# Masking the inner attention scores on VectorE instead of TensorE, in a banded attention with a product-key feed-forward

## The chip, the cores and the metric

The kernel runs on one core of a Trainium2 chip. The metric is the device time of one execution in microseconds (us): before the change, the median of three runs is 1780.42 us (1779.67 to 1784.23).

## What is computed

The reference normalizes x (16 sequences of 512 rows, 128 wide), runs attention with 16 heads of width 8 in which a query sees only keys at most 128 rows away, adds the residual, and runs a second layer (batch norm, product keys, the top 8 of 64 candidates, expert rows weighted by a softmax). Only the attention bears on the change:

```python
x = L0_attn_x
x = x + _L0_attn_ref(_layernorm(x, axis=-1), w_qkv, w_proj)
x = x + _L0_ffn_ref(_layernorm(x, axis=-1), ...)
# in _L0_attn_ref:
attn = jnp.einsum('bhqd,bhkd->bhqk', q, k) / math.sqrt(DK)
mask = jnp.abs(idx[None, :] - idx[:, None]) > WINDOW      # WINDOW = 128
attn = jnp.where(mask[None, None], -1000000000.0, attn)
p = jax.nn.softmax(attn, axis=-1)
out = jnp.einsum('bhqk,bhkd->bhqd', p, v)
```

## The kernel before

The program has two stages, one behind the other: `attention`, and then `ffn`, which the change leaves alone.

A sequence has four tiles of 128 queries. With a band of 128, the first and the last query tile see two tiles of keys each (the outer scores, PSUM tile SX, 2 x 256 columns), and the two inner ones see three tiles each (the inner scores, PSUM tile SY, 2 x 384 columns). Each of SX and SY has one buffer.

The attention is a pipeline over sequences. In the step of sequence c, a loop over the 16 heads does, for each head, on each engine in a fixed order written by hand:

- TensorE: `scores` of sequence c (SX, then SY), some of the single products and transposes that the list SHARED gives to heads (they share the one bank MB), for four of the 16 heads (2, 6, 10, 14 by VSLOT) the product with the values, `values` (16 pairs of matmuls, PV), and then `scoresT` of sequence c-1, the transposed scores less their row's maximum (TX, TY).
- VectorE: the maximum of each row of SX (L409) and of SY (L411), and between them the small work that belongs to that head: statistics and normalization (L378 to L388), the splitting of q and k into three bf16 parts (L435, L440), the division by the sums (L447, L449), the residual (L457), and the batch-norm statistics (L468).
- ScalarE: the exponentials of TX and TY (L354, L356) and copies out of MB.
- GpSimd: zeroes the entries outside the band after the exponential (L264) and computes two small powers (L272, L286).
- SP: the DMAs; q and k go through DRAM and come back, spread over partitions.

Masking of the scores that the maxima are taken of is done on TensorE. After the product of a tile, a further matmul adds a triangle of -1e30 (`bandb`, bf16) through the identity `idb`. SX needs one such matmul of 256 columns, SY four of 128 columns (two for each query tile, L492):

```python
for n, i in enumerate((1, 2)):
    tile(SY[:, n, 0:3 * P], i, i - 1, i + 2)
    outside(SY[:, n, 0:P], LO)
    o = outside(SY[:, n, 2 * P:3 * P], HI)
o.then_inc(S["inner_scores"], 1)
```

`scores` of a head waits for `outer_maxima` of the head before (SX free), and then, before SY, for `inner_maxima` of the head before (SY free). VectorE waits for `outer_scores` ahead of L409 and for `inner_scores` ahead of L411. TensorE's two transposes of the maxima (L559, L563) wait for `inner_maxima`, and the bank MB passes from one user to the next by `bank_free`.

Steps -1, 0 and 1 and steps 14 to 17 are written out; steps 2 to 13 are the body of a hardware loop of six turns, two steps in each:

```python
for t in (-1, 0, 1):
    do(t, t)
with eng.Fori(0, 6) as i:
    do(i * 2 + 2, 2)
    do(i * 2 + 3, 3)
```

Of the kernel before, what the change touches and what calls it, by code (L numbers as in the profile page):

```python
# [33 lines left out]
P = 128  # L34
# [15 lines left out]
VSUB = TILES * H // 2 * SLOT_V  # L50


def attention(nc, ctx, x, w_qkvT, w_projT, identb, band, w_q, keysT, idf, bnst, KM, extra, x1_out, x2T_out, first):
    def sb(name, shape, dt=F32):
        return ctx.enter_context(nc.sbuf_tensor(name, shape, dt))

# [17 lines left out]
    KT = sb("KT", [P, 2 * FH * NK])  # L74
    idb = sb("idb", [P, P], BF16)
    bandb = sb("bandb", [P, 2 * P], BF16)
    xin = [sb(f"xin{b}", [P, TILES, P]) for b in range(2)]
    xres = sb("xres", [P, TILES, P])
    st6 = sb("st6", [P, TILES, 6])
# [46 lines left out]


    def steps(eng, do):
        for t in (-1, 0, 1):
            do(t, t)  # L130
        with eng.Fori(0, 6) as i:
            do(i * 2 + 2, 2)
            do(i * 2 + 3, 3)
        for t in (14, 15, 16, 17):
            do(t, t)


# [31 lines left out]
    def _(sp):  # L169

        sp.dma_start(xin[0][:, :, :], xs[0]).then_inc(S["x_loaded"], 16)
        for dst, src in ((wq[:, :], w_qkvT), (wp[:, :], w_projT), (idb[:, :], identb), (bandb[:, :], band)):
            sp.dma_start(dst, src).then_inc(S["consts_loaded"], 16)
        for dst, src in extra[:1]:
            sp.dma_start(dst, src).then_inc(S["consts_loaded"], 16)
# [196 lines left out]
    def _(dve):  # L372
# [18 lines left out]
        def shift(s, nth):  # L391
# [4 lines left out]
            dve.wait_ge(S["max_part2"], s * 2 + nth)  # L396
            nc.vector.tensor_tensor(mp[:, 2, :], rm[:, :], mp[:, 1, :], ALU.subtract).then_inc(S["max_part3"], 1)

        def step(t, c):
            b = c % 2  # L400
            for h in range(H):
                if 0 <= c < SEQS:
                    n = t * H + h + 1
                    dve.wait_ge(S["outer_scores"], n)
                    if h == 0 and c >= 1:
                        dve.wait_ge(S["maxima_turned"], t * 2 - 1)
                    if h == 8 and c >= 1:
                        dve.wait_ge(S["maxima_turned"], t * 2)
                    nc.vector.tensor_reduce(mx[:, h, 0:4:3], SX[:, :, :], AX.X, ALU.max).then_inc(S["outer_maxima"], 1)  # L409
                    dve.wait_ge(S["inner_scores"], n)  # L410
                    nc.vector.tensor_reduce(mx[:, h, 1:3], SY[:, :, 0:384], AX.X, ALU.max).then_inc(S["inner_maxima"], 1)  # L411

                if h == 1 and 0 <= c - 1 < SEQS:
                    shift(t - 1, 2)
                if h == 9 and 0 <= c < SEQS:
                    shift(t, 1)

                if h == 0 and 0 <= c + 1 < SEQS:
                    dve.wait_ge(S["x_loaded"], 16 * (t + 2))
                    stats(0, t + 1, xin[1 - b], st6, mv, ve, S["x_stats"], S["x_means"], S["x_variance"])  # L420
                if h == 1 and 0 <= c + 1 < SEQS:
                    stats(1, t + 1, xin[1 - b], st6, mv, ve, S["x_stats"], S["x_means"], S["x_variance"])
                if h == 3 and 0 <= c + 1 < SEQS:
                    dve.wait_ge(S["x_rstd"], t + 2)
                    if c >= 0:
                        dve.wait_ge(S["xn_turned"], t + 1)
                    norm(xin[1 - b], mv, rs, xn, S["xn_ready"])
                if c == -1 and h in (4, 7):

                    both = K[0 if h == 4 else 1][64:P, :, :].rearrange("p h n -> p (h n)").bitcast(F32)  # L430
                    nc.vector.memset(both, TWO_ONES).then_inc(S["k_ones_set"], 1)
                for hh, nm, dst, r, sc in ((5, "q", qp, rq, DK ** -0.5), (7, "k", kp, rk, 1.0)):
                    if h == hh and 0 <= c + 1 < SEQS:
                        dve.wait_ge(S[nm + "_part1"], t + 2)
                        nc.vector.scalar_tensor_tensor(out=r[:, :].rearrange("p (i n) -> p i n", n=P), in0=MB[:, :, :], scalar=sc,  # L435
                                                       in1=dst[:, 0, :].rearrange("p (i n) -> p i n", n=P),
                                                       op0=ALU.mult, op1=ALU.subtract).then_inc(S[nm + "_rest"], 1)
                    if h == hh + 1 and 0 <= c + 1 < SEQS:
                        dve.wait_ge(S[nm + "_part2"], t + 2)
                        nc.vector.tensor_tensor(dst[:, 2, :], r[:, :], dst[:, 1, :], ALU.subtract).then_inc(S[nm + "_part3"], 1)  # L440

                for i, sl in enumerate(ASLOT):
                    if h == sl and 0 <= c - 2 < SEQS:
                        n = (t - 2) * 2 + i + 1
                        dve.wait_ge(S["att_turned"], n)
                        hv = MB[:, :, :].rearrange("p g (h e) -> p (g h) e", e=SLOT_V // 2)
                        nc.vector.reciprocal(rec[:, i, :], hv[:, :, DK]).then_inc(S["sums_inverted"], 1)  # L447
                        dve.wait_ge(S["sums_inverted"], n)
                        nc.vector.tensor_tensor(A[:, 2 * i:2 * i + 2, :].rearrange("p i (h d) -> p (i h) d", d=DK), hv[:, :, 0:DK],  # L449
                                                rec[:, i, :].unsqueeze(2).broadcast_to([P, 2 * H, DK]), ALU.mult).then_inc(S["att_normed"], 1)  # L450

                if h == 12 and 0 <= c - 2 < SEQS:
                    dve.wait_ge(S["projected"], t - 1)
                    dve.wait_ge(S["residual_loaded"], 16 * (t - 1))
                    if c - 2 >= 1:
                        dve.wait_ge(S["x1_stored"], 16 * (t - 2))
                    nc.vector.tensor_tensor(X1[:, :, :], MB[:, :, :], xres[:, :, :], ALU.add).then_inc(S["x1_ready"], 1)  # L457
                if h == 13 and 0 <= c - 2 < SEQS:
                    dve.wait_ge(S["x1_ready"], t - 1)
                    stats(0, t - 2, X1, t6, tv, te, S["x1_stats"], S["x1_means"], S["x1_variance"])  # L460
                    stats(1, t - 2, X1, t6, tv, te, S["x1_stats"], S["x1_means"], S["x1_variance"])
                if h == 14 and 0 <= c - 2 < SEQS:
                    dve.wait_ge(S["x1_rstd"], t - 1)
                    norm(X1, tv, trs, X2, S["x2_ready"])
# [6 lines left out]

    @block.tensor
    def _(pe):
        pe.wait_ge(S["consts_loaded"], 80)
        pe.wait_ge(S["v_pads_set"], 5)

        HI, LO = bandb[:, 0:P], bandb[:, P:2 * P]

        def scores(t, c, h):

# [3 lines left out]
            if h == 8:  # L484
                pe.wait_ge(S["heads_8_15_loaded"], 192 * (t + 1))

            def tile(out, i, k0, k1, clear=True):
                pe.matmul(out, Q[b][0:KQ, h, i * P:(i + 1) * P], K[b][0:KQ, h, k0 * P:k1 * P],  # L488
                          start=clear, stop=False, skip_group_check=True)

            def outside(out, band_):
                return pe.matmul(out, idb[:, :], band_, start=False, stop=True, skip_group_check=True)  # L492

            if c > 0 or h > 0:
                pe.wait_ge(S["outer_maxima"], n - 1)
            tile(SX[:, 0, :], 0, 0, 2)
            tile(SX[:, 1, :], 3, 2, 4, False)

            outside(SX[:, :, :].rearrange("p j n -> p (j n)")[:, P:3 * P], bandb[:, :]).then_inc(S["outer_scores"], 1)
            if c > 0 or h > 0:  # L500
                pe.wait_ge(S["inner_maxima"], n - 1)
            for n, i in enumerate((1, 2)):
                tile(SY[:, n, 0:3 * P], i, i - 1, i + 2)
                outside(SY[:, n, 0:P], LO)
                o = outside(SY[:, n, 2 * P:3 * P], HI)
            o.then_inc(S["inner_scores"], 1)

        def scoresT(t, c, h):

# [40 lines left out]
        def step(t, c):  # L550
            b = c % 2
            for h in range(H):
# [2 lines left out]

                if h == 1 and 0 <= c - 1 < SEQS:
                    bank_free(pe, "mt1", t, c)
                    pe.wait_ge(S["inner_maxima"], t * H)
                    pe.transpose(MB[0:HT, 0, :], mx[:, 8:16, :].rearrange("p h i -> p (h i)"), idf[:, :]).then_inc(S["maxima_turned"], 1)  # L559
                if h == 9 and 0 <= c < SEQS:  # L560
                    bank_free(pe, "mt0", t, c)
                    pe.wait_ge(S["inner_maxima"], t * H + 8)
                    pe.transpose(MB[0:HT, 0, :], mx[:, 0:8, :].rearrange("p h i -> p (h i)"), idf[:, :]).then_inc(S["maxima_turned"], 1)  # L563

                if h == 4 and 0 <= c + 1 < SEQS:
# [447 lines left out]
        outputs(GROUPS * GT - 1, GROUPS - 1, 1, GT - 1)  # L1013


def program(nc, x, w_qkvT, w_projT, ident, identb, band, w_q, keysT, key_inT, key_out, gb, out):
    x1 = nc.dram_tensor("x1", (SEQS * T, P), F32, kind="Internal").ap()
    x2T = nc.dram_tensor("x2T", (P, SEQS * T), F32, kind="Internal").ap()
    with ExitStack() as both:
# [9 lines left out]
        first = [sb("X1_first", [P, TILES, P]), sb("X2T_first", [P, T])]  # L1029
        extra = [(idf[:, :], ident), (KI[:, :], key_inT), (KO[:, :, :], key_out), (GB[:, :], gb)]  # L1030
        with ExitStack() as ctx:
            attention(nc, ctx, x, w_qkvT, w_projT, identb, band, w_q, keysT, idf, bnst, KM, extra, x1, x2T, first)
        with ExitStack() as ctx:
            ffn(nc, ctx, x1, x2T, KM, KI, KO, GB, idf, bnst, first, out)

# [35 lines left out]
```

## Time and profile before

| what | value |
|---|---|
| median of three runs | 1780.42 us |
| the profiled execution | 1781.27 us, its span 1779.6 us |
| TensorE busy | 1539.2 us (86%), 11712 matmuls |
| VectorE busy | 1477.4 us (83%) |
| ScalarE busy | 1266.0 us (71%) |
| GpSimd busy | 1328.7 us (75%) |
| mean granted TensorE clock | 0.953 of full speed |

PE is TensorE's matmuls, PEld its weight loads, DVE VectorE, ACT ScalarE, POOL GpSimd, SPq the queue that issues the DMAs. A row `[x <-E T Lnnn]` says that the engine stood idle for x us before the instruction, until line nnn of engine E, which writes T, had ended. The busy time of a matmul runs from its start to a modelled end, so that matmuls in a row overlap; what one takes from its successor is seen from start to start. VectorE's instructions also overlap by a little. The attention fills the first 780 us of the span, the feed-forward the rest.

### The profile page before, as it was taken

What the parts mean: (1) busy time and instruction counts of PE and PEld (TensorE: products, weight loads), DVE (VectorE), ACT (ScalarE), POOL (GpSimd) and SP (SyncE); (2) the same over time, 40 slices, a digit from 0 to 9 for tenths busy, and PEclk for the clock granted to TensorE, in tenths of its full rate; (3) what the DMA queues carried; (4) which work ended last, traced back from release to release, by engine and by line L of the source; (5) the groups of instructions that cost most, each with busy time, mean ns of one, the idle gap of its engine ahead of it and who ended that gap; (6) DMA issues with size and microseconds to landing.
All of it is one profiled execution on the core that took longest, in us unless ns stands there. A gap on an engine that the chain in (4) does not pass through costs nothing.

```text
span 1779.6 us, 35628 instructions
## 1 busy us (share of the span) xinstructions
PE 1539.2 (86%) x11712; PEld 1100.6 (62%) x11712; DVE 1477.4 (83%) x3720; ACT 1266.0 (71%) x1741; POOL 1328.7 (75%) x1579
## 2 busy tenths in 40 slices
PE   3899999999999999868888888888888888888887
PEld 2455655656555665426666676766666676766666
DVE  3767888888878887339999999999999999999998
ACT  1156666666666666638888888888888888888885
POOL 1045555555555555639999999999999999999993
PEclk9789999999999999969999999999999999999999
DMA  5334444444444443010000000000000000000000
GB/s 143 78 82 93 101 101 99 100 97 97 97 97 105 97 97 84 27 54 1 19 18 2 19 19 1 19 19 19 1 19 19 9 10 19 19 1 19 13 7 7
DMA packets 73436, 85.62 MB, mean 48 GB/s; under 512 B 9856, under 2 KB 63616, under 8 KB 68608
## 3 DMA queue, kind: packets, MB, share of 16 engines
q1 hardware_dynamic: 73312, 84.08, 20.1%
q8 instruction: 64, 1.05, 0.3%
q14 instruction: 60, 0.49, 0.1%
HBM read 58.10 MB, written 25.95 MB: 47 GB/s over the span
## 4 chain that ended last, share of the span: by engine, by line
POOL 31%; issue 7%; DVE 7%; ACT 6%; PE 5%; DVEq 0%; ACTq 0%; SPq 0%
POOL SUM L746 31%; DVE W L939 5%; PE WT L1007 3%; ACT E L847 3%; ACT L781 1%; PE MB L949 1%; ACT GE L780 1%; DVE M8Y L883 0%; PE MB L952 0%; DVE SMALL L900 0%; ACT SIM L774 0%; PE MB L974 0%; DVE CT L922 0%; PE E L962 0%; ACT OUT L794 0%
## 5 line engine op out<-in xcount | busy, mean ns | idle before, releaser
L746 POOL TENSOR_TENSOR SUM<-SIM 128x1024 f32<-128x1024 f32 x512 | 958.0, 1913 | 9.5 <-DVE W L939 5.5
L939 DVE SCALAR_TENSOR_TENSOR W<-SUM,SMALL,E 128x1024 f32<-128x1024 f32 x512 | 641.6, 1279 | 45.8 <-ACT E L847 43.8
L847 ACT ACTIVATE E<-SUM,NB 128x1024 f32<-128x1024 f32 x512 | 566.8, 1118 | 100.1 <-DVE W L939 89.8
L1007 PEld LDWEIGHTS WT<-idf,W 128*128 128x128 f32 x4096 | 488.7, 149 | 237.9 <-DVE W L939 124.3
L1007 PE MATMUL WT<-idf,W 128*128 128x128 f32 x4096 | 559.9, 288 | 70.8 <-DVE CT L922 38.0
L264 POOL TENSOR_SCALAR_AFFINE_SELECT PT<-PT 128x128 f32<-128x128 f32 (+1 forms) x1024 | 334.6, 351 | 319.4 <-ACT PT L354 283.0
L409 DVE TENSOR_REDUCE mx<-SX 128x2 f32<-128x512 f32 x256 | 175.3, 685 | 105.1 <-PE SX L492 104.3
L411 DVE TENSOR_REDUCE mx<-SY 128x2 f32<-128x768 f32 x256 | 242.4, 947 | 7.3 <-PE SY L492 6.9
L354 ACT ACTIVATE PT<-TX 128x512 f32<-128x512 f32 x256 | 152.9, 597 | 98.5 <-PE TX L519 97.1
L356 ACT ACTIVATE PT<-TY 128x768 f32<-128x768 f32 x256 | 207.2, 809 | 1.5
L488 PE MATMUL SY<-K,Q 72*128 72x384 bf16 x512 | 164.0, 343 | 16.4 <-DVE mx L411 15.7
L545 PE MATMUL PV<-PT,V 128*32 128x384 f32 (+1 forms) x2048 | 154.7, 444 | 2.3 <-POOL PT L264 2.3
L492 PE MATMUL SY<-bandb,idb 128*128 128x128 bf16 x1024 | 146.7, 225 | 0.0
L949 PE MATMUL MB<-KM,BNT 128*128 128x512 f32 x128 | 79.5, 706 | 70.9 <-ACT OUT L794 69.1
L519 PE MATMUL TY<-Q,K 75*128 75x384 bf16 x512 | 127.2, 330 | 6.2 <-ACT PT L356 6.2
L492 PEld LDWEIGHTS SY<-bandb,idb 128*128 128x128 bf16 x1024 | 104.1, 102 | 40.5 <-issue 6.4
L974 PE MATMUL MB<-KO,CT 128*128 128x128 f32 x1024 | 124.9, 275 | 1.1 <-DVE CT L922 1.1
L974 PEld LDWEIGHTS MB<-KO,CT 128*128 128x128 f32 x1024 | 119.5, 192 | 1.3 <-DVE CT L922 1.3
L488 PE MATMUL SX<-K,Q 72*128 72x256 bf16 x512 | 103.1, 284 | 14.2 <-DMA Q<-q_parts 12.4
L545 PEld LDWEIGHTS PV<-PT,V 128*32 128x32 f32 x2048 | 60.8, 111 | 72.8 <-issue 53.5
L519 PE MATMUL TX<-Q,K 75*128 75x256 bf16 x512 | 100.3, 277 | 5.1 <-DMA Q<-m_parts 3.5
L922 DVE TENSOR_TENSOR CT<-WT,GE 128x1024 f32<-128x1024 f32 x64 | 78.3, 1224 | 17.6 <-PE WT L1007 17.6
(111 smaller groups left out, 1663.3 us busy)
## 6 DMA issues: line engine op xcount, KB each, us to landing
K<-k_parts SPq DMA_DIRECT2D x96, 192.0 KB
Q<-q_parts SPq DMA_DIRECT2D x288, 64.0 KB
q_parts<-qp SPq DMA_DIRECT2D x16, 384.0 KB, 2.4
k_parts<-kp SPq DMA_DIRECT2D x16, 384.0 KB, 2.4
xin<-in_x SPq DMA_DIRECT2D x16, 256.0 KB, 3.1
xres<-in_x SPq DMA_DIRECT2D x16, 256.0 KB, 9.4
x<-X SPq DMA_DIRECT2D x16, 256.0 KB, 2.2
x2T<-X2T SPq DMA_DIRECT2D x16, 256.0 KB, 2.1
```

Source lines behind the costliest of these rows:

```text
L264: return nc.gpsimd.affine_select(out=out, in_=out, compare_op=ALU.is_ge, fill=0.0, base=0, pattern=([[0, 2]] if pairs else []) + [[s, P]], ...
L356: nc.scalar.activation(pt[:, 512:1280].rearrange("p (j n) -> p j n", j=2), TY[:, :, 0:384], ACT.Exp).then_inc(S["inner_exp"], 1)
L411: nc.vector.tensor_reduce(mx[:, h, 1:3], SY[:, :, 0:384], AX.X, ALU.max).then_inc(S["inner_maxima"], 1)
L488: pe.matmul(out, Q[b][0:KQ, h, i * P:(i + 1) * P], K[b][0:KQ, h, k0 * P:k1 * P], start=clear, stop=False, skip_group_check=True)
L492: return pe.matmul(out, idb[:, :], band_, start=False, stop=True, skip_group_check=True)
L519: return pe.matmul(out[:, 0:(q1 - q0) * P], K[b][0:R, h, j * P:(j + 1) * P], Q[b][0:R, h, q0 * P:q1 * P], start=True, stop=True, skip_grou ...
L545: o = pe.matmul(PV[32 * e:32 * e + 32, q0 * P:q1 * P], V[b][:, slot:slot + SLOT_V], PT[:, h % 8, at:at + (q1 - q0) * P], start=(j == 0 and ...
L746: return eng.tensor_tensor(SUM[(q * FH + h) % RING][:, :].rearrange("p (i j) -> p i j", i=NK), sx, sy, ALU.add)
L847: nc.scalar.activation(E[h % 2][:, :], SUM[(k * FH + h) % RING][:, :], ACT.Exp, bias=NB[q][:, h:h + 1]).then_inc(S["exp_ready"], 1)
L939: nc.vector.scalar_tensor_tensor(out=W[h % WRING][:, :], in0=SUM[(k * FH + h) % RING][:, :], scalar=TOP[q][:, h, TOPK - 1:TOPK], in1=E[h % ...
L974: o = pe.matmul(po, CT[k % 2][:, e, :], key_out[:, e, :], start=False, stop=(e == BLK - 1))
L1007: o = pe.matmul(WT[:, e, :], W[h % WRING][:, e * P:(e + 1) * P], ident[:, :], is_transpose=True, start=(h == 0 and e % 4 == 0), stop=(h == ...
```

## The change

- The four matmuls that add the triangles to SY are gone. The product of each of the two inner query tiles now ends its own group and raises `inner_scores` by itself, so that this semaphore goes up twice for a head.
- VectorE's L411, one maximum over both inner tiles, becomes two `tensor_tensor_reduce`, one for each tile: the instruction adds a mask `bandf` (fp32, SBUF, 384 columns: triangle, zeros, triangle) to the scores, writes the sum back to SY, and leaves the row's maximum in `mx`. Each waits for its own tile and raises `inner_maxima`, which now also goes up twice; `scores` waits for each half of SY by itself.
- `bandf` is a new constant of 128 x 384 fp32, loaded with the other constants; TensorE and VectorE wait for all six of them (96) where TensorE waited for five (80).
- All steps of the attention are written out; the hardware loop is gone.

SX keeps its mask matmul and its L409.

```diff
+    bandf = sb("bandf", [P, 3 * P])
...
     def steps(eng, do):
-        for t in (-1, 0, 1):
-            do(t, t)
-        with eng.Fori(0, 6) as i:
-            do(i * 2 + 2, 2)
-            do(i * 2 + 3, 3)
-        for t in (14, 15, 16, 17):
+        for t in range(-1, SEQS + 2):
             do(t, t)
...
-        for dst, src in ((wq[:, :], w_qkvT), (wp[:, :], w_projT), (idb[:, :], identb), (bandb[:, :], band)):
+        for dst, src in ((wq[:, :], w_qkvT), (wp[:, :], w_projT), (idb[:, :], identb), (bandb[:, :], band), (bandf[:, :], bands)):
             sp.dma_start(dst, src).then_inc(S["consts_loaded"], 16)
...
+        def masked_max(scores, k0, k1, out):
+
+            return nc.vector.tensor_tensor_reduce(out=scores, in0=scores, in1=bandf[:, k0 * P:k1 * P], scale=1.0,
+                                                  scalar=-3e38, op0=ALU.add, op1=ALU.max, accum_out=out)
+
+        dve.wait_ge(S["consts_loaded"], 96)
...
-                    dve.wait_ge(S["inner_scores"], n)
-                    nc.vector.tensor_reduce(mx[:, h, 1:3], SY[:, :, 0:384], AX.X, ALU.max).then_inc(S["inner_maxima"], 1)
+                    dve.wait_ge(S["inner_scores"], 2 * n - 1)
+                    masked_max(SY[:, 0, 0:3 * P], 0, 3, mx[:, h, 1:2]).then_inc(S["inner_maxima"], 1)
+                    dve.wait_ge(S["inner_scores"], 2 * n)
+                    masked_max(SY[:, 1, 0:3 * P], 0, 3, mx[:, h, 2:3]).then_inc(S["inner_maxima"], 1)
...
-        pe.wait_ge(S["consts_loaded"], 80)
+        pe.wait_ge(S["consts_loaded"], 96)
...
-            if c > 0 or h > 0:
-                pe.wait_ge(S["inner_maxima"], n - 1)
-            for n, i in enumerate((1, 2)):
-                tile(SY[:, n, 0:3 * P], i, i - 1, i + 2)
-                outside(SY[:, n, 0:P], LO)
-                o = outside(SY[:, n, 2 * P:3 * P], HI)
-            o.then_inc(S["inner_scores"], 1)
...
+            for e, i in enumerate((1, 2)):
+                if c > 0 or h > 0:
+                    pe.wait_ge(S["inner_maxima"], 2 * n - 3 + e)
+                tile(SY[:, e, 0:3 * P], i, i - 1, i + 2).then_inc(S["inner_scores"], 1)
...
-                    pe.wait_ge(S["inner_maxima"], t * H)
+                    pe.wait_ge(S["inner_maxima"], t * H * 2)
...
-                    pe.wait_ge(S["inner_maxima"], t * H + 8)
+                    pe.wait_ge(S["inner_maxima"], t * H * 2 + 16)
```

## Rows read from the trace of the kernel before

**Rows 1.** The page: busy time of each engine, and the granted clock in 40 slices

```profile
PE 1539.2 (86%) x11712; PEld 1100.6 (62%) x11712; DVE 1477.4 (83%) x3720; ACT 1266.0 (71%) x1741; POOL 1328.7 (75%) x1579
...
PEclk9789999999999999969999999999999999999999
```

**Rows 2.** Busy time by stretch: window, length, busy us (instructions), clock, DMA share, GB/s

```profile
80.00:124.00 44.00, 42.24 (x324) 25.61 (x322) 30.57 (x54) 25.27 (x43) 20.67 (x63) 0.82 0.37 81
...
218.84:261.90 43.06, 40.25 (x382) 25.71 (x378) 35.05 (x73) 26.65 (x47) 22.88 (x67) 1.00 0.45 99
```

**Rows 3.** Timeline of GpSimd, one fixed instruction of three successive steps: start, us, instruction

```profile
596.83 1.01 POOL L286 TENSOR_TENSOR trs<-te,half 128x4 f32<-128x4 f32 x1
...
639.88 1.01 POOL L286 TENSOR_TENSOR trs<-te,half 128x4 f32<-128x4 f32 x1
...
682.92 1.01 POOL L286 TENSOR_TENSOR trs<-te,half 128x4 f32<-128x4 f32 x1
```

**Rows 4.** Timeline of VectorE in one looped step

```profile
433.48 0.38 DVE L382 BATCH_NORM_AGGREGATE mv<-st 128x2 f32<-128x6 f32 x4
...
436.81 0.69 DVE L409 TENSOR_REDUCE mx<-SX 128x2 f32<-128x512 f32 x1 [1.25 <-PE SX L492]
...
439.72 0.42 DVE L449 TENSOR_TENSOR A<-MB,rec 128x256 f32<-128x256 f32 x1
...
448.05 0.69 DVE L409 TENSOR_REDUCE mx<-SX 128x2 f32<-128x512 f32 x1 [1.25 <-PE SX L492]
...
450.15 0.69 DVE L435 SCALAR_TENSOR_TENSOR rk<-MB,kp 128x512 f32<-128x512 f32 x1 [0.55 <-ACT kp L313]
450.75 0.68 DVE L409 TENSOR_REDUCE mx<-SX 128x2 f32<-128x512 f32 x1
451.35 0.95 DVE L411 TENSOR_REDUCE mx<-SY 128x2 f32<-128x768 f32 x1
452.22 0.68 DVE L440 TENSOR_TENSOR kp<-rk,kp 128x512 bf16<-128x512 f32 x1
...
453.54 0.68 DVE L409 TENSOR_REDUCE mx<-SX 128x2 f32<-128x512 f32 x1
...
459.18 0.69 DVE L409 TENSOR_REDUCE mx<-SX 128x2 f32<-128x512 f32 x1 [1.80 <-PE SX L492]
...
462.56 0.69 DVE L457 TENSOR_TENSOR X<-MB,xres 128x512 f32<-128x512 f32 x1
463.44 0.69 DVE L409 TENSOR_REDUCE mx<-SX 128x2 f32<-128x512 f32 x1 [0.18 <-PE SX L492]
...
468.67 1.12 DVE L388 TENSOR_SCALAR X<-X,tv,trs 128x128 f32<-128x128 f32 x4 [0.58 <-POOL trs L286]
...
474.25 0.67 DVE L409 TENSOR_REDUCE mx<-SX 128x2 f32<-128x512 f32 x1
474.84 0.95 DVE L411 TENSOR_REDUCE mx<-SY 128x2 f32<-128x768 f32 x1
```

**Rows 5.** Timeline of TensorE in the same step

```profile
440.27 0.65 PE L569 MATMUL MB<-idf,xn 128*128 128x128 f32 x4 [1.07 <-DVE A L449]
...
453.68 0.28 PE L563 MATMUL MB<-idf,mx 128*32 128x128 f32 x1 [0.59 <-DVE A L449]
...
455.14 0.34 PE L488 MATMUL SY<-K,Q 72*128 72x384 bf16 x1 [0.30 <-DVE mx L411]
455.31 0.28 PE L492 MATMUL SY<-bandb,idb 128*128 128x128 bf16 x2
455.43 0.33 PE L488 MATMUL SY<-K,Q 72*128 72x384 bf16 x1
...
475.85 0.34 PE L488 MATMUL SY<-K,Q 72*128 72x384 bf16 x1 [0.36 <-DVE mx L411]
```

**Rows 6.** Timeline of the start: a constant's DMA issue, and TensorE's first work

```profile
2.79 0.43 SPq L173 DMA_DIRECT2D bandb<-in_band  x1
...
7.71 1.09 PE L569 MATMUL MB<-idf,xn 128*128 128x128 f32 x4 [7.71 <-DVE xn L388]
```

More of the change, by code:

```diff
@@ L50, with attention @@
 VSUB = TILES * H // 2 * SLOT_V
-def attention(nc, ctx, x, w_qkvT, w_projT, identb, band, w_q, keysT, idf, bnst, KM, extra, x1_out, x2T_out, first):
+def attention(nc, ctx, x, w_qkvT, w_projT, identb, band, bands, w_q, keysT, idf, bnst, KM, extra, x1_out, x2T_out, first):
     def sb(name, shape, dt=F32):
@@ L473, in _ @@
     def _(pe):
-        pe.wait_ge(S["consts_loaded"], 80)
+        pe.wait_ge(S["consts_loaded"], 96)
         pe.wait_ge(S["v_pads_set"], 5)
-        HI, LO = bandb[:, 0:P], bandb[:, P:2 * P]
         def scores(t, c, h):
@@ L485, in scores, with tile @@
                 pe.wait_ge(S["heads_8_15_loaded"], 192 * (t + 1))
[L487 to L492, printed above, removed]
+            def tile(out, i, k0, k1, clear=True, done=True):
+                return pe.matmul(out, Q[b][0:KQ, h, i * P:(i + 1) * P], K[b][0:KQ, h, k0 * P:k1 * P],
+                                 start=clear, stop=done, skip_group_check=True)
             if c > 0 or h > 0:
                 pe.wait_ge(S["outer_maxima"], n - 1)
-            tile(SX[:, 0, :], 0, 0, 2)
-            tile(SX[:, 1, :], 3, 2, 4, False)
-            outside(SX[:, :, :].rearrange("p j n -> p (j n)")[:, P:3 * P], bandb[:, :]).then_inc(S["outer_scores"], 1)
-            if c > 0 or h > 0:
-                pe.wait_ge(S["inner_maxima"], n - 1)
-            for n, i in enumerate((1, 2)):
-                tile(SY[:, n, 0:3 * P], i, i - 1, i + 2)
-                outside(SY[:, n, 0:P], LO)
-                o = outside(SY[:, n, 2 * P:3 * P], HI)
-            o.then_inc(S["inner_scores"], 1)
+            tile(SX[:, 0, :], 0, 0, 2, done=False)
+            tile(SX[:, 1, :], 3, 2, 4, clear=False, done=False)
+            pe.matmul(SX[:, :, :].rearrange("p j n -> p (j n)")[:, P:3 * P], idb[:, :], bandb[:, :],
+                      start=False, stop=True, skip_group_check=True).then_inc(S["outer_scores"], 1)
+            for e, i in enumerate((1, 2)):
+                if c > 0 or h > 0:
+                    pe.wait_ge(S["inner_maxima"], 2 * n - 3 + e)
+                tile(SY[:, e, 0:3 * P], i, i - 1, i + 2).then_inc(S["inner_scores"], 1)
         def scoresT(t, c, h):
@@ L1013, in _, with program @@
         outputs(GROUPS * GT - 1, GROUPS - 1, 1, GT - 1)
-def program(nc, x, w_qkvT, w_projT, ident, identb, band, w_q, keysT, key_inT, key_out, gb, out):
+def program(nc, x, w_qkvT, w_projT, ident, identb, band, bands, w_q, keysT, key_inT, key_out, gb, out):
     x1 = nc.dram_tensor("x1", (SEQS * T, P), F32, kind="Internal").ap()
@@ L1031, in program @@
         with ExitStack() as ctx:
-            attention(nc, ctx, x, w_qkvT, w_projT, identb, band, w_q, keysT, idf, bnst, KM, extra, x1, x2T, first)
+            attention(nc, ctx, x, w_qkvT, w_projT, identb, band, bands, w_q, keysT, idf, bnst, KM, extra, x1, x2T, first)
         with ExitStack() as ctx:
@@ L1056 @@
         "band": np.concatenate([np.where(keep.T, 0, -1e30), np.where(keep, 0, -1e30)], axis=1).astype(ml_dtypes.bfloat16),
+        "bands": np.concatenate([np.where(keep, 0, -1e30), np.zeros((P, P)), np.where(keep.T, 0, -1e30)], axis=1).astype(np.float32),
         "w_q": np.asarray(L0_ffn_w_q),
```

## The prediction

> **What bounds the kernel now.** I read the page first: TensorE is busy for 86% of the span, VectorE for 83%, and no engine stands out [rows 1]. The change touches only the attention, so I cut that stage into windows. A steady step of it takes 43.06 us, of which TensorE is busy for 40.25 and VectorE for 35.05, at full clock [rows 2]. Neither fills the step, so the next views are the timelines of both engines in one step, to see who waits for whom. They take turns. Ahead of L409 of heads 3, 7 and 11 (at 436.81, 448.05 and 459.18) VectorE stands idle for 1.25, 1.25 and 1.80 us until TensorE has the outer scores [rows 4]; these are the heads behind the long product with the values. In other places TensorE stands idle until VectorE is done: 1.07 us at L569, 0.59 at L563, 0.30 and 0.36 at the first tile of SY [rows 5]. The step is thus a chain that changes engines: pieces that go by VectorE's work and pieces that go by TensorE's.
>
> **The price of each part.**
>
> TensorE loses four matmuls for each head. Two of them stand between 455.31 and 455.43, 0.12 us from start to start, with rounding 0.115 [rows 5]. That is 0.23 us a head, 3.7 us in a step of 16 heads, where TensorE's is the piece that counts. Its busy time of 0.28 for the pair is not the price.
>
> VectorE trades one maximum over 768 columns for two masked ones over 384. L409 with 512 columns takes 0.60 us from its start to the next start (450.75 to 451.35), L411 with 768 takes 0.87 (451.35 to 452.22) [rows 4]. The slope is 0.27 us for 256 columns, so 384 columns take 0.60 - 0.135 = 0.465. Two make 0.93, which is x = 0.06, say 0.07 us a head more than L411. The second source, in SBUF, costs nothing by L457, which reads PSUM and SBUF and lasts 0.69 for 512 columns, as L409 does [rows 4]. No row shows an operation that writes a tensor and a maximum besides, so that I bound it. Below: nothing, x = 0.07. A likely value: one more small instruction for each. Four of L382 last 0.38 us in all, a single one some 0.16, so that they start (0.38 - 0.16) / 3 = 0.075 apart [rows 4]; x = 0.07 + 0.15 = 0.22. Above: the small instruction starts only when the masked one has quite ended (0.08 later, since L409 lasts 0.68 and its successor starts after 0.60), and runs its 0.16 out: x = 2 x (0.465 + 0.08 + 0.16) - 0.87 = 0.54. I take 0.22, because VectorE's instructions without a wait between them overlap throughout rows 4. The Trainium skill speaks against the change here: "VectorE: DVE Perf Modes", section "Two Vector instructions with no wait between them", treats an op that also writes out its accumulator as two instructions. No run here shows it yet; by that rule x = 0.22 or more, without it 0.07 and some 20 us less in all.
>
> Nor does a row show VectorE reading and writing one PSUM bank in the same instruction. If a column then took two cycles, x would be 0.22 + 2 x 384 x 1.05 ns = 1.03. The outputs of L409, L411 and L457 go to SBUF. This end is kept as a rival.
>
> Now along the chain of one step, with x for each head on a VectorE piece and -0.23 on a TensorE piece [rows 4, 5]:
>
> - 436.81 to 440.27, head 3: VectorE's L409, L411, norms, L449, and then TensorE's L569: +x = +0.22.
> - 440.27 to 448.05: TensorE's; the masks of heads 5 and 6 fall out: -0.46.
> - 448.05 to 453.54: at head 7, L435 waits 0.55 us for a product that stands behind head 7's masks: -0.23; head 8 is VectorE's: +x. Together -0.01.
> - 453.54 to 459.18: the first tile of SY waits for L411 (455.14), and behind it stand both tiles and four masks. Now the first tile is filled while VectorE reads the second half, and only one tile (0.17) is left behind the second. That saves 0.23 for the masks and 0.17 or 0.18 for the tile: x - 0.41 = -0.19.
> - 459.18 to 463.44, heads 11 and 12: TensorE's, -0.46; but VectorE's own work there is 4.26 less the waits ahead of the two L409, 0.4 and 0.25, so that with 2x it takes 4.05. It becomes the bound: -0.20.
> - 463.44 to 475.85, heads 13 to 1: VectorE's. Head 14 hides its x under the 0.58 us for which L388 waits for GpSimd; heads 13, 15, 0 and 1 pay: +4x; some 0.2 of a wait for a copy at head 15 goes, as TensorE is earlier; at 475.85 the tiles of SY gain 0.41 as above: 4x - 0.61 = +0.27.
>
> The sum is -0.37 us a step, with x = 0.22. For the 14 steps of sequences 2 to 15 that makes -5.2 us. In general the pieces add up to 9x - 2.35, which is zero at x = 0.26: the change stands close to where it turns. With x = 0.07 heads 11 and 12 stay TensorE's, and the sum is -1.68 a step, -23.5 us; with 0.54 L435 of head 7 is no longer earlier either, and it is +2.7, +38 us.
>
> Sequences 0 and 1 run in part at a lower clock: the stretch from 80 to 124 had 0.82 of full speed [rows 2], which is full speed for some of it and half for the rest. There a mask costs twice as much, 0.46 us a head, and TensorE is busy 42.24 of 44.00. For some ten heads at half clock, 4.6 us, and x against it in about seven others, 1.5, I put -3 us.
>
> The new constant is 192 KB, one more DMA issue, 0.48 us behind the others on SP's queue, and TensorE waits for it. Its first work was at 7.71, released by VectorE's norms, while the issue of `bandb` was done at 3.22 [rows 6]; two more issues and the landing come close to that. I put +0.5, between 0 and 1.5. The loads of xin and of the feed-forward's tables are one issue later too; their first use comes later, so nothing.
>
> Writing out the steps costs or gives nothing. The instruction L286 of successive steps stands at 596.83, 639.88 and 682.92: the last looped step took 43.05, the first written-out one 43.04 [rows 3]. The second stage is the same. The Trainium skill, "Runtime: NRT & Kernel Launch", section "Instruction fetch mechanics", says that a taken branch can force a fetch and that kernels prefer full unrolling; the trace shows no such gain here, 0.01 us a step, 0.1 us in all.
>
> The sum: -5.2 - 3 + 0.5 = -7.7 against the profiled 1781.27 us, whose span was 1779.6. The median of the runs is 0.85 lower: 1780.42 - 7.7 = 1772.7, say 1773 us.
>
> **The rivals.**
>
> The second output is dear. VectorE would have x from 0.3 to 0.54, if the write of the maximum doesn't overlap with its neighbours. For it: three ALU steps and two outputs in one instruction, an operation no row shows. Against it: everything small on VectorE overlaps. It decides from x = 0.26 upward; at 0.4 the sum is +1.3 us a step, 1780.4 + 18 - 2.5 = 1796; at 0.54, 1816. Chance 0.20. This is the one that ends on the other side.
>
> The bank's two accesses halve the rate. VectorE's 35 us of a step would become 35 + 16.5 = 51.5, the bound of every head, 52 with waits: +9 for 16 steps, 1925 us. Chance 0.05.
>
> The clock falls. TensorE has 3.7 us less to do in a step and stands idle more often. Now it holds full speed in each steady step [rows 2], but the page's slices at the start, in which it works less, show 7 and 8 [rows 1]. If some 3 us of each step ran at half speed on a TensorE piece, that would be +1.5 a step, +21: 1794 us. Chance 0.10.
>
> The second output is free, x = 0.07: 1780.4 - 23.5 - 3 + 0.5 = 1754 us. Chance 0.12.
>
> The change does nothing: what VectorE takes and TensorE gives cancel, since a wait gone on one engine comes back at the next (the waits for ScalarE and GpSimd stay). 1778 us. Chance 0.08.
>
> **How the numbers follow.** My forecast, x from 0.15 to 0.28, has 0.45, and the time 1773. Its own range is 1764 to 1779. The measurement tells changes from about 0.3%, 5.3 us, so the forecast is faster below 1775.1: 0.35 of its 0.45, and 0.10 within. With the free output that makes 0.47 faster; within 0.3% come 0.10, 0.08 for nothing, and 0.03 from the edge of the rivals: 0.21; slower is the rest, 0.32. The range of 1757 to 1803 leaves out the half rate, the upper part of the dear output and some of the free one, 2 in 10 in all.
>
> **What would show it.** In the trace after: 1024 matmuls less in all; the pair of masked maxima taking 1.09 us from the start of the first to the start of what follows (0.87 now; 0.94 if the second output is free, over 1.2 if it is dear, 1.9 at half rate); L409's waits at heads 3, 7 and 11 still there; L569's wait longer (1.07 + 0.45), because VectorE is now later and TensorE earlier; a steady step of 42.7 us; clock 1.00 in it; the written-out steps alike. I am wrong if the pair's price is outside 0.93 to 1.15, if a steady step shows a lower clock, or if heads 4, 11 and 12 turn into VectorE's and the small TensorE savings vanish.

## The result, and the profile after

The changed kernel takes 1801.12 us (median of 15 runs, 1782.63 to 1805.96) against 1780.01 us (15 runs); the ratio is 1.0097, with a 95% interval of 1.0075 to 1.0118. It is slower, by 1%. I had forecast 1773 us, and faster. The measured time lies within the stated range, but the change moved the time the other way. Ratios here compare runs in the usual state alone; one of the ten runs of half_masks took 2418 us at a granted clock of 0.56 and is left out of its ratio.

The profiled execution took 1802.2 us, its span 1800.5, which is 20.9 us more than before. The page, as in [rows 1]:

```profile
PE 1540.5 (86%) x10688; PEld 1049.4 (58%) x10688; DVE 1509.5 (84%) x4488; ACT 1264.7 (70%) x1741; POOL 1334.4 (74%) x1579
...
PEclk9679999899989999878999999999999999999999
```

TensorE has 1024 matmuls less and is busy for as long as before. That is the sign to stop at. In the row of the clock the attention's slices, all 9 before once the start was over, now show 8 here and there: TensorE was granted full speed for a part of the time only.

What VectorE's new instructions take, from its timeline at head 8 of a step (start, us, instruction), beside L409, L411 and L440 of [rows 4], which are L412, L397 and L445 now:

```profile
280.95 0.68 DVE L412 TENSOR_REDUCE mx<-SX 128x2 f32<-128x512 f32 x1
281.55 0.56 DVE L397 CUSTOM_DVE_ANT_0 SY<-SY,bandf 128x384 f32<-128x384 f32 x1
282.02 0.14 DVE L397 DVE_READ_ACCUMULATOR2_ANT mx<- 128x1 f32 x1
282.02 0.60 DVE L397 CUSTOM_DVE_ANT_0 SY<-SY,bandf 128x384 f32<-128x384 f32 x1
282.54 0.14 DVE L397 DVE_READ_ACCUMULATOR2_ANT mx<- 128x1 f32 x1
282.54 0.69 DVE L445 TENSOR_TENSOR kp<-rk,kp 128x512 bf16<-128x512 f32 x1
```

The pair takes 282.54 - 281.55 = 0.99 us from start to start; L411 took 0.87. So x is 0.12 us a head. The maximum is written out by an instruction of its own (0.14 us). That is as the Trainium skill has it ("VectorE: DVE Perf Modes", section "Two Vector instructions with no wait between them"): an op with an accumulator output is two instructions. But it runs beside the next one: each of them starts when its successor starts. The first masked maximum takes 0.47 us to the next start, the second 0.52, so that the cost beyond the rate of a plain maximum is some 0.05 us.

How long the steps are, by GpSimd's L282 (L286 of [rows 3]) in two parts of the stage:

```profile
389.07 1.01 POOL L282 TENSOR_TENSOR trs<-te,half 128x4 f32<-128x4 f32 x1
430.72 1.01 POOL L282 TENSOR_TENSOR trs<-te,half 128x4 f32<-128x4 f32 x1
474.04 1.01 POOL L282 TENSOR_TENSOR trs<-te,half 128x4 f32<-128x4 f32 x1
518.40 1.01 POOL L282 TENSOR_TENSOR trs<-te,half 128x4 f32<-128x4 f32 x1
...
607.71 1.01 POOL L282 TENSOR_TENSOR trs<-te,half 128x4 f32<-128x4 f32 x1
652.10 1.01 POOL L282 TENSOR_TENSOR trs<-te,half 128x4 f32<-128x4 f32 x1
697.05 1.01 POOL L282 TENSOR_TENSOR trs<-te,half 128x4 f32<-128x4 f32 x1
```

Steps of 41.65, 43.32, 44.36, 44.39 and 44.95 us: one kernel, written-out steps with the same instructions, 3.3 us apart. Before, they were 43.05 and 43.04 [rows 3]. The windows of the first and of the third of these steps say what differs (columns as in [rows 2]; the clock stands behind the last count):

```profile
389.07:430.72 41.65, 37.80 (x322) 21.59 (x314) 37.06 (x121) 26.52 (x46) 23.32 (x68) 1.00 0.46 104
474.04:518.40 44.36, 40.69 (x321) 22.47 (x314) 36.67 (x120) 26.55 (x46) 23.32 (x67) 0.92 0.43 99
```

At full speed a step takes 41.65 us, 1.4 less than before. With a mean clock of 0.92, which is some 7 of the 44.36 us at half speed (1.2 GHz instead of 2.4), it takes 2.7 us more than that. Of the twelve steps between the first and the last row of this kind (167.91 and 697.05), the one at 389.07 alone had the clock at 1.00; two had 0.96 and nine 0.92.

The last three rows of GpSimd stand 10.9, 12.2 and 14.1 us behind those of before [rows 3]. The 20.9 us of the span are thus 1.7 up to the first of these rows, 12.4 in the twelve steps, 4.3 in the last steps of the attention and 2.5 in the feed-forward. Of the last two little is the change's: in the last steps both_masks and before_flat (below), at the time of the kernel before, are 3.3 and 1.9 us longer too, and before_flat is 2.4 longer in the feed-forward.

Where the half speed bites is seen on both engines' timelines around head 10 of a slow step (from 255.63 to 300.04). TensorE:

```profile
284.00 0.28 PE L561 MATMUL MB<-idf,mx 128*32 128x128 f32 x1 [0.93 <-DVE A L454]
284.12 0.57 PE L517 MATMUL TX<-Q,K 75*128 75x256 bf16 x2
284.50 0.84 PE L517 MATMUL TY<-Q,K 75*128 75x384 bf16 x2
...
286.55 4.50 PE L543 MATMUL PV<-PT,V 128*32 128x256 f32 x32
290.98 0.39 PE L517 MATMUL TX<-Q,K 75*128 75x256 bf16 x2
```

and VectorE:

```profile
286.30 0.67 DVE L412 TENSOR_REDUCE mx<-SX 128x2 f32<-128x512 f32 x1
...
292.07 0.69 DVE L412 TENSOR_REDUCE mx<-SX 128x2 f32<-128x512 f32 x1 [4.05 <-PE SX L499]
```

Behind its wait of 0.93 us TensorE goes on at half speed (the pair of TX lasts 0.57 where it lasts 0.39 at 290.98), and the product with the values, the longest piece that is TensorE's alone, takes 4.50 us. VectorE, which waited 1.80 us at this place before [rows 4], waits 4.05. The same instructions in the step at full speed, with a values product of head 6 in front:

```profile
408.59 2.36 PE L543 MATMUL PV<-PT,V 128*32 128x256 f32 x32
...
417.45 0.28 PE L561 MATMUL MB<-idf,mx 128*32 128x128 f32 x1 [0.93 <-DVE A L454]
417.57 0.38 PE L517 MATMUL TX<-Q,K 75*128 75x256 bf16 x2
```

The product takes 2.36 us there. The wait of 0.93 us is the same to the hundredth, and this time the speed stays, so that no single wait decides.

### The profile page after: what moved, and what is told of

The parts are those of the page before. It is cut to its first block, busy times and chain, and to the rows that moved or that the text cites. A ratio compares the mean times of both kernels' runs of the same rounds, so it can differ in the third digit from the quotient of the medians.

```text
span 1800.5 us, 33004 instructions
## 1 busy us (share of the span) xinstructions
PE 1540.5 (86%) x10688; PEld 1049.4 (58%) x10688; DVE 1509.5 (84%) x4488; ACT 1264.7 (70%) x1741; POOL 1334.4 (74%) x1579
## 4 chain that ended last, share of the span: by engine, by line
POOL 41%; issue 5%; ACT 4%; DVE 3%; PE 2%; DVEq 0%; ACTq 0%; SPq 0%
POOL SUM L744 41%; DVE W L937 2%; ACT E L845 2%; ACT L779 1%; PE WT L1005 1%; ACT GE L778 1%; PE MB L947 0%; PE MB L972 0%; PE E L960 0%; DVE M8Y L881 0%; DVE SMALL L898 0%; ACT L778 0%; DVE CT L920 0%; ACT SIM L772 0%; PE MB L950 0%
## 5 line engine op out<-in xcount | busy, mean ns | idle before, releaser
L1005 PEld LDWEIGHTS WT<-idf,W 128*128 128x128 f32 x4096 | 494.3, 151 | 234.2 <-DVE W L937 120.7
L1005 PE MATMUL WT<-idf,W 128*128 128x128 f32 x4096 | 566.3, 291 | 69.4 <-DVE CT L920 38.0
L260 POOL TENSOR_SCALAR_AFFINE_SELECT PT<-PT 128x128 f32<-128x128 f32 (+1 forms) x1024 | 340.2, 357 | 328.9 <-ACT PT L350 293.1
L397 DVE CUSTOM_DVE_ANT_0 SY<-SY,bandf 128x384 f32<-128x384 f32 x512 | 273.9, 576 | 0.0
L412 DVE TENSOR_REDUCE mx<-SX 128x2 f32<-128x512 f32 x256 | 175.1, 684 | 106.2 <-PE SX L499 105.7
L543 PE MATMUL PV<-PT,V 128*32 128x384 f32 (+1 forms) x2048 | 177.7, 495 | 2.3 <-POOL PT L260 2.3
L491 PE MATMUL SY<-K,Q 72*128 72x384 bf16 x512 | 152.2, 356 | 6.9 <-DVE mx L397 6.1
L517 PE MATMUL TY<-Q,K 75*128 75x384 bf16 x512 | 132.6, 342 | 6.9 <-ACT PT L352 6.7
L543 PEld LDWEIGHTS PV<-PT,V 128*32 128x32 f32 x2048 | 66.0, 122 | 100.2 <-issue 86.5
L491 PEld LDWEIGHTS SX<-K,Q 72*128 72x128 bf16 x512 | 49.9, 102 | 69.9 <-DVE mx L412 21.3
L491 PEld LDWEIGHTS SY<-K,Q 72*128 72x128 bf16 x512 | 52.2, 102 | 55.6 <-DVE mx L397 48.4
```

The lines of the kernel that those rows point to most:

```text
L260: return nc.gpsimd.affine_select(out=out, in_=out, compare_op=ALU.is_ge, fill=0.0, base=0, pattern=([[0, 2]] if pairs else []) + [[s, P]], ...
L397: return nc.vector.tensor_tensor_reduce(out=scores, in0=scores, in1=bandf[:, k0 * P:k1 * P], scale=1.0, scalar=-3e38, op0=ALU.add, op1=ALU ...
L491: return pe.matmul(out, Q[b][0:KQ, h, i * P:(i + 1) * P], K[b][0:KQ, h, k0 * P:k1 * P], start=clear, stop=done, skip_group_check=True)
L517: return pe.matmul(out[:, 0:(q1 - q0) * P], K[b][0:R, h, j * P:(j + 1) * P], Q[b][0:R, h, q0 * P:q1 * P], start=True, stop=True, skip_grou ...
L543: o = pe.matmul(PV[32 * e:32 * e + 32, q0 * P:q1 * P], V[b][:, slot:slot + SLOT_V], PT[:, h % 8, at:at + (q1 - q0) * P], start=(j == 0 and ...
L1005: o = pe.matmul(WT[:, e, :], W[h % WRING][:, e * P:(e + 1) * P], ident[:, :], is_transpose=True, start=(h == 0 and e % 4 == 0), stop=(h == ...
```

## The experiments

Theory 1, formed on this profile: the change does what it should in the chain, but it takes so much work from TensorE that it is granted half speed in most steps, and that costs more than the chain gains. Theory 2: the masked maxima are what costs, VectorE sets the steps. All runs are timed against the kernel before on the same chip.

**The masks put back, beside the masked maxima (both_masks).**

```diff
-                tile(SY[:, e, 0:3 * P], i, i - 1, i + 2).then_inc(S["inner_scores"], 1)
+                tile(SY[:, e, 0:3 * P], i, i - 1, i + 2, done=False)
+                pe.matmul(SY[:, e, 0:P], idb[:, :], bandb[:, P:2 * P], start=False, stop=True, skip_group_check=True)
+                pe.matmul(SY[:, e, 2 * P:3 * P], idb[:, :], bandb[:, 0:P], start=False, stop=True,
+                          skip_group_check=True).then_inc(S["inner_scores"], 1)
```

> The changed kernel, with the four mask matmuls of each head put back ahead of the masked maxima (the mask is then added twice, with the same maxima). TensorE has the work of before, VectorE that of the changed kernel. Theory 1, the clock: the changed kernel is slow because TensorE, with less work, is granted half speed for 6.8 us in most steps. With the masks back the clock stays at 1.00 in the steady steps, and the kernel gets faster though it does more: steady step 43.5 us, time 1785 to 1790. Theory 2, VectorE: the masked maxima cost 0.24 us a head more, and that sets the step. Then more work can't help: steady step 44.4 or more, time 1801 or above.

1781.67 us, ratio 1.0007 (0.9993 to 1.0022). A step in the windows:

```profile
292.17:335.21 43.04, 40.55 (x382) 25.98 (x378) 37.27 (x121) 26.60 (x46) 23.30 (x68) 1.00 0.47 102
```

A kernel that does strictly more than the changed one is 1% faster, with the clock at 1.00 in all twelve steps. Theory 2 is out. And beside TensorE's old work the masked maxima cost hardly anything: 43.04 us a step, where before_flat, the next run, has 42.94.

**Written-out steps alone (before_flat).** The edit is the change's second hunk, on the kernel before.

> The kernel before with all steps written out and nothing else. As predicted, no effect: steady step 43.05 us at clock 1.00, ratio 1.000 within 0.003. If writing out were what changed the granted clock, half-speed stretches would show in the steady steps here too, and the time would be near 1800.

1781.0 us, ratio 0.9999 (0.9986 to 1.0012).

```profile
336.57:379.51 42.94, 40.31 (x382) 25.70 (x378) 34.95 (x73) 26.58 (x46) 22.92 (x67) 1.00 0.45 102
```

No effect on the time, none on the clock. The step is 0.1 us shorter than the looped one, some 1.4 us in twelve steps, which the total doesn't show.

**TensorE's relief alone (no_inner_mask).** On the written-out kernel before:

```diff
             for n, i in enumerate((1, 2)):
-                tile(SY[:, n, 0:3 * P], i, i - 1, i + 2)
-                outside(SY[:, n, 0:P], LO)
-                o = outside(SY[:, n, 2 * P:3 * P], HI)
+                o = pe.matmul(SY[:, n, 0:3 * P], Q[b][0:KQ, h, i * P:(i + 1) * P], K[b][0:KQ, h, (i - 1) * P:(i + 2) * P],
+                              start=True, stop=True, skip_group_check=True)
             o.then_inc(S["inner_scores"], 1)
```

> The kernel before, written out, with the four mask matmuls of each head left out and the maximum taken by the one reduction of before: the maximum runs over all three key tiles, inside the band or not (softmax allows any shift). VectorE's price is thus nothing, TensorE's relief is that of the changed kernel. Theory 1: TensorE is idle more often than before, half-speed stretches appear in steady steps here as well; at full clock a step would be 40.5 to 41, with the stretches 42.5 to 43.5, time 1765 to 1785. Theory 2: no clock effect, the whole relief is seen: step 41 us at most in every step, time 1750 or below.

1775.01 us (1766.74 to 1791.78), ratio 0.9967 (0.9934 to 1.0000). Five of the twelve steps had the full clock, the others took 42.7 to 45.9 us. One of each:

```profile
338.26:379.31 41.05, 37.13 (x321) 21.12 (x314) 34.83 (x73) 26.46 (x46) 23.11 (x67) 1.00 0.45 106
251.33:297.21 45.88, 42.06 (x322) 22.90 (x314) 34.98 (x73) 26.71 (x46) 23.06 (x68) 0.89 0.44 96
```

The half speed comes without any masked maximum, once TensorE has less to do. But this kernel is no slower than the one before: in its profiled execution five steps kept the full clock, against one in the changed kernel, and why the masked maxima make that worse is not shown. With before_flat and both_masks this takes the full-clock step apart: relief alone 42.94 to 41.05, -1.89 us; the masked maxima alone +0.10; both 41.65, so that beside the relief the maxima, with the waits that come in two halves, cost 0.60.

**Half of the masks (half_masks).** The changed kernel, with the two mask matmuls put back for the first inner tile only (`e == 0`).

> The changed kernel with the two mask matmuls of the first inner tile put back, those of the second left out: TensorE's work stands half-way between the changed kernel and the run with all four back. At full clock a step should take 42.3 us (between 41.65 and 43.03). Theory 1: half-speed stretches are rarer than in the changed kernel but not gone, time 1780 to 1795. Theory 2, without a clock effect: half-way between 1801 and 1781, 1791, with clock 1.00.

1776.3 us, ratio 0.9977 (0.9961 to 0.9993).

```profile
335.92:377.84 41.92, 38.56 (x354) 24.07 (x350) 37.11 (x121) 26.58 (x46) 23.13 (x67) 1.00 0.47 102
250.39:294.00 43.61, 40.49 (x354) 24.36 (x350) 37.10 (x121) 26.58 (x46) 23.09 (x68) 0.96 0.44 101
```

The half speed is rarer and shorter (0.96 for 0.92 in an affected step, and nine of the twelve steps have none). The total is lower than I expected of theory 1, and lower than that of either neighbour: less work than before, and little of the clock lost.

**Matmuls of zeros where TensorE waits (fill_idle, fill_more).** A matmul of zeros into PV, without a start flag, adds nothing:

```diff
+        def fill(n):
+            for _ in range(n):
+                pe.matmul(PV[:, :], ZB[:, 0:P], ZB[:, :], start=False, stop=True, skip_group_check=True)
...
                 if h == 9 and 0 <= c < SEQS:
+                    if c >= 2:
+                        fill(4)
                     bank_free(pe, "mt0", t, c)
...
                 if h == 4 and 0 <= c + 1 < SEQS:
+                    if c >= 2:
+                        fill(6)
                     bank_free(pe, "xnT", t, c)
```

> The changed kernel, with matmuls of zeros into PV (512 columns each, they add nothing) where TensorE waits for VectorE anyway: six at head 4 (it waits 1.5 us there) and four at head 9 (1.1 us). Theory 1: the half-speed stretch at head 10 goes or gets rarer, steady step 41.7 us where the clock is 1.00; if it goes in all steps, 14 steps x 2.8 us less, time about 1765. Theory 2: no gain, 1801, as these matmuls shorten nothing.

1779.84 us (1771.93 to 1787.24), ratio 0.9988 (0.9969 to 1.0008). Two of its steps:

```profile
434.38:476.02 41.64, 39.68 (x330) 22.42 (x324) 37.04 (x121) 26.41 (x46) 23.46 (x67) 1.00 0.46 106
256.24:303.13 46.89, 43.56 (x331) 23.89 (x324) 37.25 (x121) 26.64 (x46) 23.47 (x67) 0.89 0.46 96
```

Better than the changed kernel by 1%, but not what I expected if theory 1 held in all steps: five of the twelve steps had the full clock. Half speed was gone from head 10 and came up in heads 0 to 2. In the slow step above it set in behind two waits for DMAs that bring back parts of Q from DRAM, 0.78 us and then 1.80, both at head 0, and took in the values product of head 2:

```profile
263.14 0.61 PE L523 MATMUL TX<-Q,K 75*128 75x256 bf16 x2 [1.80 <-DMA Q<-m_parts]
...
268.16 4.36 PE L549 MATMUL PV<-PT,V 128*32 128x256 f32 x32
```

That step is 5.2 us longer than the other, but the two waits are in it besides the clock. The second run spreads the zeros:

```diff
+FILL = {15: 2, 0: 2, 1: 2, 4: 6, 8: 2, 9: 4}
...
                 if 0 <= c < SEQS:
                     scores(t, c, h)
+                    if c >= 1:
+                        fill(FILL.get(h, 0))
```

> The changed kernel with matmuls of zeros into PV (512 columns each, they add nothing) from sequence 1 on, at each head at which TensorE was seen to wait for VectorE: two each at heads 15, 0, 1 and 8, six at head 4, four at head 9, behind the scores; 18 in a step, about 3.8 us of TensorE. With ten at heads 4 and 9 alone the half-speed stretches became rarer and moved to heads 15 to 1. Theory 1, the clock: they go from the steady steps, the step is 41.6 to 42.2 us, clock 1.00, time 1760 to 1768. Theory 2, TensorE's added work eats what the clock gives: step 43, time 1780.

1762.97 us (four runs), ratio 0.9898 (0.9874 to 0.9921), and the steps are those of the chain:

```profile
414.66:456.29 41.63, 40.76 (x337) 23.08 (x332) 37.04 (x121) 26.52 (x46) 23.43 (x67) 1.00 0.48 103
```

18 matmuls added to each step, 38 us of the median gone. One steady step of the profiled execution still had a half-speed stretch (45.9 us); it too has two waits for these DMAs ahead of it, of 0.66 and 1.13 us. The other eleven took 41.6 to 41.8.

**The control: the same zeros where the clock is full anyway (before_fill).** The written-out kernel before with the 18 matmuls.

> A control: the kernel before, written out, with its masks and with the same 18 matmuls of zeros in a step. Its steady steps had full speed already. If the zeros help only through the clock, they can give nothing here, and the step grows by what of them isn't hidden: 43.0 to 44.0, time 1780 to 1795. If they helped in another way (order, waits), this kernel would get faster too, by some 1%.

1786.15 us, ratio 1.0018 (1.0002 to 1.0034):

```profile
380.23:423.60 43.37, 42.93 (x397) 27.76 (x396) 34.90 (x73) 26.59 (x46) 22.81 (x67) 1.00 0.45 100
```

The step is 0.43 us longer than without them. Where the clock is full anyway the zeros give nothing. In fill_more they left the full-clock step as it was (41.63 for 41.65) and raised the share of such steps from one to eleven in twelve, so that their gain there is the clock's.

**Faster than both kernels (nomask_fill, nomask_fill_early, nomask_all_fill).** The maximum in a softmax may be any number near the largest score, so that the mask isn't needed for it as long as no score outside the band is so far above those inside that every exponential of the row becomes zero; inputs of that kind were not run. The kernel without inner masks got the 18 matmuls:

> The kernel before, written out, without the four mask matmuls (the maximum over all three key tiles by one reduction), with the same 18 matmuls of zeros. Without them a step took 41.05 us at full clock and 44.3 to 45.9 with a half-speed stretch. Theory 1: clock 1.00 in the steady steps, step 41.1 to 41.8, time 1752 to 1762. Theory 2: 1775 to 1780.

1753.11 us (four runs, 1751.15 to 1760.60), ratio 0.986 (0.9828 to 0.9892), with all twelve steps at clock 1.00.

```profile
405.92:446.99 41.07, 40.13 (x336) 22.95 (x332) 34.86 (x73) 26.52 (x46) 23.09 (x68) 1.00 0.46 108
```

Then zeros at the start too, `elif c == 0 and h >= 8: fill(4)`:

> As the one before, and in the step of sequence 0 four more matmuls of zeros behind the scores of heads 8 to 15, where TensorE ran at half speed and waited for VectorE and for the loads of q and k. Theory 1: the clock is at full speed earlier in the step of sequence 1, 2 to 5 us less than the run without them. Theory 2: they only lengthen head by head at half speed (0.43 us each), 5 us more.

1758.69 us (four runs, 1753.60 to 1764.36), ratio 0.9882 (0.9847 to 0.9916): no gain, and the intervals overlap. The first of GpSimd's rows, L285 here, stood at 163.1 us, 4 us later than without them. But it was not the added matmuls that took these 4 us, as theory 2 had it. Of the values products behind them, first in nomask_fill, then in nomask_fill_early:

```profile
116.91 2.36 PE L548 MATMUL PV<-PT,V 128*32 128x256 f32 x32
126.38 2.36 PE L548 MATMUL PV<-PT,V 128*32 128x256 f32 x32
...
116.58 2.36 PE L548 MATMUL PV<-PT,V 128*32 128x256 f32 x32
129.38 3.33 PE L548 MATMUL PV<-PT,V 128*32 128x256 f32 x32
```

At 117 us the kernel with the zeros was 0.3 us ahead; then a half-speed stretch came, which the other execution had not (clock 0.73 and 1.00 from 120 to 130 us). The start differs by 2 or 3 us between executions of the same instructions, half speed included (next section), so that this pair doesn't tell what the zeros at the start are worth. And without the mask of the outer scores (its matmul of 256 columns left out, `outer_scores` raised by the second tile):

> The fastest so far (no mask matmuls on the inner scores, one plain maximum, 18 matmuls of zeros), and in addition the mask matmul of the outer scores left out: its maximum too runs over keys outside the band. TensorE is relieved by another 0.11 us a head. If the clock holds, the step is 40.5 to 40.9 us (41.07 with that mask), time 1743 to 1750; if the lower load brings the half-speed stretches back, 1755 to 1765.

1750.51 us (four runs, 1749.38 to 1751.34), ratio 0.9816 (0.9788 to 0.9844), the fastest. The interval touches that of nomask_fill, so the order of these two isn't settled. Two of its steps:

```profile
442.93:484.24 41.31, 38.98 (x317) 21.56 (x316) 35.03 (x73) 26.55 (x46) 23.00 (x67) 1.00 0.48 105
524.94:565.64 40.70, 38.96 (x317) 21.56 (x316) 34.94 (x73) 26.54 (x46) 23.04 (x67) 1.00 0.49 107
```

The clock was full in all twelve. Nine took 40.7 us; in the three of 41.3 to 42.5 TensorE waits 1.3 to 1.4 us for the DMA that fills Q from `m_parts` (0.9 at most in the others), so that at this speed the reload begins to show.

## Why the prediction was wrong

**The step that failed** is the sentence on the clock. I counted every steady step at full speed, as before, and gave the falling clock a chance of 0.10. It was the case that came: eleven of the twelve steady steps ran in part at half speed. My price for it was right in kind and low: 3 us of each step at half speed, +1.5, 1794 us; the trace shows about 7 us in an affected step, +2.7, and 1801 us. I had the sign of it in hand: the start, in which TensorE gets fewer matmuls done (324 in 44.00 us, where a steady step has 382), ran in part at half speed [rows 1, 2], and the change takes 3.7 us of work, by my price, from the 40.25 of a step and makes TensorE wait longer for VectorE. What I took as evidence against, full speed in every steady step, only said that the old load was enough. That 1801 us lies within my range of 1757 to 1803 is no merit of the forecast: the upper part of it stood for a dear second output, which didn't come.

**VectorE's price.** x = 0.22 was forecast, with 0.07 and 0.54 as the ends; it is 0.12. The rate of the plain maximum held (0.47 us from start to start for 384 columns, as worked out from L409 and L411), reading and writing one bank halves nothing, and the read of the maximum overlaps. So the rivals of the dear output and of the half rate fell.

**The chain.** With x = 0.12 in place of 0.22 the formula 9x - 2.35 gives -1.27 us a step; the full-clock step has -1.4. L412 of the heads at which I cut the chain, in that step (to be read beside [rows 4]):

```profile
401.13 0.69 DVE L412 TENSOR_REDUCE mx<-SX 128x2 f32<-128x512 f32 x1 [0.80 <-PE SX L499]
...
411.97 0.69 DVE L412 TENSOR_REDUCE mx<-SX 128x2 f32<-128x512 f32 x1 [0.97 <-PE SX L499]
...
422.74 0.69 DVE L412 TENSOR_REDUCE mx<-SX 128x2 f32<-128x512 f32 x1 [1.28 <-PE SX L499]
...
426.70 0.68 DVE L412 TENSOR_REDUCE mx<-SX 128x2 f32<-128x512 f32 x1
```

Heads 3 to 7 take 10.84 us (11.24 before), heads 7 to 11 10.77 (11.13), heads 11 and 12 3.96 (4.26), and the rest of the step 16.08 (16.4): -0.40, -0.36, -0.30 and some -0.35. I had -0.24, -0.20, -0.20 and +0.27. With x = 0.12 the pieces would be -0.34, -0.40, -0.41 and -0.13: the first two fit, the third is 0.1 off, and the last 0.2. The sum comes out in part because these two errors go against each other. The last piece was VectorE's by my count; I haven't taken it further apart. The waits at heads 3, 7 and 11 are still there, as forecast, and shorter. TensorE's wait at L567 (L569 before) grew, by less than I said:

```profile
404.62 0.66 PE L567 MATMUL MB<-idf,xn 128*128 128x128 f32 x4 [1.36 <-DVE A L454]
```

1.36 for 1.07 [rows 5].

**Writing out the steps** does nothing to the time, as forecast; the step is 0.1 us shorter where I had 0.01. The rule of the Trainium skill that speaks for it ("Runtime: NRT & Kernel Launch", section "Instruction fetch mechanics") has at most that much here.

**The constant** is a term that I mis-sized: +0.5, between 0 and 1.5. The kernel before, and then the changed one:

```profile
3.69 0.88 DVE L378 BATCH_NORM_STATS2 st<-xin 128x6 f32<-128x128 f32 x4 [3.69 <-DMA xin<-in_x]
...
6.40 0.87 DVE L374 BATCH_NORM_STATS2 st<-xin 128x6 f32<-128x128 f32 x4 [6.40 <-DMA idf<-in_ident]
...
10.41 1.09 PE L567 MATMUL MB<-idf,xn 128*128 128x128 f32 x4 [10.41 <-DVE xn L384]
```

TensorE's first work came at 10.41 us where it had come at 7.71 [rows 6], 2.7 later. I had counted the wait of TensorE for the constants and overlooked that VectorE now waits for all six of them too, ahead of its first norms, which had needed `xin` alone. In the runs with `bandf` and no zeros ahead of it this first matmul stands at 10.1 to 10.4, in before_flat and no_inner_mask, without `bandf`, at 8.0 and 7.7.

**The start** I had at -3 for sequences 0 and 1. GpSimd's first L282 came at 167.9 us, where L286 had come at 166.2, 1.7 us later, constant included, with half speed in more of it (0.74 for 0.82 in the window from 80 to 124 us, [rows 2]). One execution of each doesn't size the term: before_flat has 164.7, both_masks 163.1. And fill_idle, which up to its first zeros at 136.6 us is the changed kernel but for a memset, has 164.3; its values product ahead of the zeros stood at 130.2 us, where the changed kernel's stood at 132.7. So the start moves by 2 or 3 us from one execution to the next, with the half speed in it, and neither the size of this term nor its sign is settled.

**What spreads the times.** Before, 15 runs lay within 9.4 us; of the changed kernel they lie 23 us apart, and they go with the mean clock: 1782.63 us at 0.939, 1805.96 at 0.925. The gain of the chain is there where the clock holds: fill_more, with full clock in eleven of twelve steps, took 1762.97 us, zeros included.

**What stays open**: what exactly TensorE must do to keep full speed. In the changed kernel half-speed stretches came behind several waits near each other and none longer than 1.4 us, in fill_idle also behind one of 1.8; they came in some steps and not in others of the same kernel, with the same waits; nomask_all_fill kept the full clock through waits of 1.2 and 1.4 us 2.6 us apart; and the stretches moved when zeros filled one place. The runs don't give a threshold. The Trainium skill, "TensorE: Matmul & The Clock Gate", section "A second HAM failure mode: psum-queue depth-cycling", tells of short idle times between groups of matmuls, frequent enough to make the clock go back and forth. The traces here agree in kind, with waits of 0.9 and 1.4 us, and don't show that it is the same mechanism.

## What to carry to other kernels

Work taken from TensorE isn't only time given back. Count what it will do afterwards, and look at stages of the same trace that are loaded less; if they show half speed, the saving may be paid back. Here it was 1.7 to 3.3 us in each step with such a stretch, against a gain of 1.4. A busy time that stays the same with 9% fewer matmuls is the first thing that shows it.

Places where TensorE waits anyway can be filled with matmuls of zeros at little cost (18 in a step: nothing in fill_more, 0.43 us in before_fill), and that was worth 38 us. A new wait that one engine gets for a constant can hold up another behind it. And before a mask is made cheaper, ask whether its result is needed: the maximum of a softmax needs none while the scores outside the band stay near those inside.

## What the hardware showed that I had not expected

A VectorE instruction that writes a tensor and a maximum has a second instruction of 0.14 us for the maximum, and it starts together with the next one. Adding a mask from SBUF, writing back to the same PSUM bank and keeping a maximum takes 0.47 us from start to start for 384 columns, the rate of a plain maximum.

TensorE's granted clock fell to half in steps in which, up to that point, it had waited at most some 1.4 us at a time, and held in another step of the same kernel with the same waits. In the kernel before it held in every steady step, with waits up to 1.07 us, and in nomask_all_fill with waits of 1.41. Matmuls of zeros kept it up in eleven of twelve steps, so it doesn't take data other than zero for that.
